# The perceptron's second product made token by token: squares become the stationary operand, weights are streamed

## The chip, the core and the metric

The kernel runs on one core of a Trainium2 chip. The metric is the device time of the whole program in microseconds. Three runs of the kernel before took 3518.9, 3522.17 and 3524.16 us; the median is 3522.17.

The core has five engines that run at the same time, each working off its own list of instructions in order: TensorE (PE in the rows; PEld are its weight loads), VectorE (DVE), ScalarE (ACT), GpSimd (POOL) and SyncE (SP), which issues the transfers. They wait for each other through semaphores.

## What is computed

Input `x` is 16 sequences of 1024 tokens with 256 values each. Two layers follow each other, each a layer norm, an attention `s` and a gate `g`, added as `x + s * silu(g)`. The first layer is a recurrent gated linear attention with a mixture of experts as gate, the second a windowed attention with a perceptron as gate. The change is in that perceptron only:

```python
def _bitlinear(x, w_latent):
    scale = clip(mean(abs(w_latent), axis=1, keepdims=True), 1e-05, None)
    tern = clip(round(w_latent / scale), -1.0, 1.0)
    return x @ (tern * scale).T            # forward value

h = _bitlinear(x, w_fc) + gate * (x @ v.T @ fast_b.T @ u.T)
r = maximum(h, 0.0)
return _bitlinear(r * r, w_proj)           # w_proj: (256, 1024)
```

Its result, 256 values for each token, goes through silu and is multiplied by the attention's output.

## The kernel before

A loop runs over the 16 sequences, eight of them unrolled in its body. The next sequence's first steps (layer norm, turning, low-rank and query products: the `head_...` helpers) are woven into the end of the current one. P is 128, D 256, KD = D/P = 2, MT = 8 (tiles of the hidden 1024), NG = 2 (halves of 512 tokens), NC = 8 (chunks of 128 tokens). Arrays are kept "turned" (features on the partitions, tokens along the row) where TensorE is to sum over features, and by token where values are normalised, gated and stored.

The perceptron is a loop over n = 0 to 15, that is over half g = n // 8 and hidden tile m = n % 8, and each engine has its own copy of it, written out by hand, several steps apart:

- TensorE: `hidden(n)` (L1837) makes hidden tile m for 512 tokens in a bank (4 matmuls of a high and a low part, one of rank 16). Three steps later `project(n - 3)` (L1861) adds this tile's share to the 256 outputs, held turned in banks 5 and 6, one per 128 outputs. Between them stand steps of the next sequence's head. The last three `project` stand behind the loop, among `head_project`, `head_route` and `head_queries`.
- ScalarE: `relus(n)` (L1089) from the bank to SBUF with the first weights' scale, then `squares(n - 1)` (L1068), the rounding of the square to fp32r, `sq_hi`.
- GpSimd: the square itself (L847).
- VectorE: `sq_lo = sq - sq_hi` (L1448), and between these `head_stats`, `head_normalise` (two chunks each at n = 6 to 9), `head_low_split`, and `finish2`.

When half g is summed up, ScalarE's `ffn_scaled(g)` (L1074, at n = 10 for the first half, behind the loop for the second) copies banks 5 and 6 to `ft` with the scale of the second weights, which is one number per output, that is per partition of the turned result. TensorE's `ffn_turn(c)` (L1876) turns `ft` back by token, two transposes for each chunk of 128 tokens, at n = 11 to 14 for the first half and among `head_queries` for the second. ScalarE's `ffn_tanh(c)` (L1082) and VectorE's `finish2(c)` (L1424: `f_gates`, `sf`, `x`) read the turned bank and complete the chunk, and SyncE stores it.

Two guards matter later. `project(8)`, the first of the second half, overwrites banks 5 and 6 and waits for both parts of `ft`. And at the next sequence's start TensorE's turning of `gates` (L1541) overwrites banks 0 and 1 and waits until ScalarE has done `experts_relu(0)` and `(1)` (L887); ScalarE gets to those behind the last `ffn_tanh`, the exponentials and logarithms of L870 and L879, and two copies. GpSimd's first step of a sequence, `parity_queries(0)` (L753), waits for `head_queries_out(1)` on ScalarE (L449). VectorE's end of a sequence runs: `head_gate` 0 to 2 (L457), `head_logits`, `head_gate(3)`, `finish2(4)`, `finish2(5)`, `head_top`, `finish2(6)`, `head_index`, `finish2(7)`.

Of the kernel before, what the change touches and what calls it, by code (L numbers as in the profile page):

```python
# [16 lines left out]
ALU = mybir.AluOpType  # L17
# [26 lines left out]
BIG = -1e30  # L44
DV = 2 * DH
UNROLL = 8


def build_program(nc, a, out, n_seq):
# [115 lines left out]
    scale_pj = sb("scale_pj", [P, KD])  # L165
    thr = sb("thr", [P, 2, MT])
# [33 lines left out]
    ft = kt[:, :, 0:512]  # L200
# [74 lines left out]
    for k in range(KD):  # L275
# [11 lines left out]
             "relu_ok sq_ok sqh_ok sql_ok pj_ok ft_ok ftp_ok tf2_ok f3_ok f4_ok y2_ok gkh_ok gkl_ok nst_ok nve_ok nrs_ok "  # L287
# [14 lines left out]
    for count, signals in (  # L302
# [4 lines left out]
            (4, "gkl_ok ve2 rs2 zexp_ok zln_ok qk2_ok xt_ok ft_ok zabs_ok gk_ok gkh_ok v2_ok z_ok "  # L307
# [7 lines left out]
             "cum_ok vg_ok f_ok ot_ok otok_ok ytp_ok s_ok pv_ok xp_ok o2tp_ok s2p_ok ftp_ok"),  # L315
# [21 lines left out]
    ffn_banks = (4, 7, 4, 7, 2, 3, 2, 3)  # L337

# [73 lines left out]
    def head_project(pe, p, where="body"):  # L412

        pe.wait_ge(s["zlo_ok"], at("zlo_ok", p // 2 + 1))
        if where == "before":
            pe.wait_ge(s["xt_ok"], at("xt_ok", NC // 2))
        elif p == 3:
            pe.wait_ge(s["f3_ok"], at("f3_ok", 4))
        else:
            pe.wait_ge(s["relu_ok"], at("relu_ok", NG * MT - 2 + p))  # L420
# [14 lines left out]
    def head_queries(pe, half, where="body"):  # L435

        if half:
            pe.wait_ge(s["z_ok"], at("z_ok", 3))
        elif where == "body":
            pe.wait_ge(s["f3_ok"], at("f3_ok", 3))  # L440
# [36 lines left out]
    with nc.Block() as block:  # L477
# [61 lines left out]
        def _(dve):  # L539
# [15 lines left out]
            for nat, ter, scale, n, width in ((fc_nat[:], fc_ter, scale_fc, MT, D), (pj_nat, pj_ter, scale_pj, KD, HID)):  # L555
# [5 lines left out]
                for m in range(n):  # L561
                    link(nc.vector.tensor_scalar(ter[:, m, :], nat[:, m, :], thr[:, 1, m:m + 1], None, ALU.is_lt))
                    link(nc.vector.scalar_tensor_tensor(ter[:, m, :], nat[:, m, :], thr[:, 0, m:m + 1],
                                                        ter[:, m, :], ALU.is_gt, ALU.subtract))
            link(nc.vector.reciprocal(rscale[:], scale_fc[:]))
# [54 lines left out]
    with nc.Block() as block:  # L620

        @block.tensor
        def _(pe):
# [17 lines left out]
            for m in range(0, MT, 4):  # L641
                turn([u_st[:, m + j, :] for j in range(4)])

        @block.scalar
        def _(act):
# [3 lines left out]
            for n, target in enumerate(targets):  # L649
                act.wait_ge(tern_pe, n + 1)  # L650
                nc.scalar.copy(target, bank[2 + n % 4][:]).then_inc(tern_act, 1)

# [58 lines left out]
    with nc.Fori(0, n_seq // UNROLL) as turn:  # L711
        with nc.Block() as block:
# [141 lines left out]
            def _(act):  # L854
                for copy in range(UNROLL):
# [218 lines left out]
                    def ffn_scaled(g):  # L1074
                        act.wait_ge(s["pj_ok"], at("pj_ok", (g + 1) * MT))
                        if g:
                            act.wait_ge(s["ftp_ok"], at("ftp_ok", 4 * g))
                        for o in range(KD):
                            nc.scalar.activation(ft[:, o, :], bank[5 + o][:], ACT.Identity, scale=scale_pj[:, o:o + 1])\
                              .then_inc(s["ft_ok"], 1)  # L1080

                    def ffn_tanh(c):  # L1082
                        act.wait_ge(s["ftp_ok"], at("ftp_ok", c + 1))
                        if c:
                            act.wait_ge(s["f3_ok"], at("f3_ok", c))
                        nc.scalar.activation(tanh_f[:], bank[ffn_banks[c]][:, 0:D], ACT.Tanh, scale=0.5)\
                          .then_inc(s["tf2_ok"], 1)
# [16 lines left out]
                    for n in range(3, NG * MT + 2):  # L1104
# [10 lines left out]
                        if n == MT + 2:  # L1115
                            ffn_scaled(0)
                        if MT + 3 <= n < MT + 7:
                            ffn_tanh(n - MT - 3)
                    ffn_scaled(1)
# [13 lines left out]
            def _(dve):  # L1133
                for copy in range(UNROLL):
# [288 lines left out]

                    def finish2(c):  # L1424
# [4 lines left out]
                        nc.vector.scalar_tensor_tensor(f_gate, tanh_f[:], 1.0, bank[ffn_banks[c]][:, 0:D],  # L1429
# [9 lines left out]
                    for n in range(NG * MT + 1):  # L1439
                        if n == MT + 5:  # L1440
# [28 lines left out]
                    head_logits(dve)  # L1469
                    head_gate(dve, 3)  # L1470
# [9 lines left out]
            def _(pe):  # L1480
                for copy in range(UNROLL):
# [29 lines left out]
                    def experts_down(i):  # L1511
# [10 lines left out]
                        elif i == 2:  # L1522
                            pass
                            if copy:
                                pe.wait_ge(s["f3_ok"], at("f3_ok"))
# [335 lines left out]
                    def project(n):  # L1861
# [113 lines left out]
```

## Time and profile before

| | |
|---|---|
| median of three runs | 3522.17 us |
| the profiled execution | 3520.74 us |
| its span, first to last instruction | 3519.0 us |
| TensorE busy, matmuls | 3365.3 us (96%) |
| TensorE busy, weight loads | 2272.8 us (65%) |
| VectorE busy | 2584.2 us (73%) |
| ScalarE busy | 1868.9 us (53%) |
| GpSimd busy | 1286.4 us (37%) |
| TensorE clock granted, mean | 0.996 of full |

A matmul's duration is the time until its last result is written, and the next one begins before that; so what a matmul costs TensorE is read from the distance between two starts, not from its length. In the same way operations on the other engines start a little before the one ahead has ended. A time "in us from the span's start" is where a row lies; one sequence takes about 213.5 us, and the rows below are from the first one's end and the second one's start.

### The profile page before, as it was taken

The page shows a single profiled execution, that of the slowest core. Times are in us where ns is not written, and L with a number is a line of the kernel's source. Part 1 is how long each engine was busy: PE and PEld are TensorE (multiplying, and loading weights), DVE is VectorE, ACT ScalarE, POOL GpSimd, SP SyncE. Part 2 cuts the span into 40 slices and gives each one's busy share as a digit, 9 for nine tenths or more (in the row PEclk, how much of TensorE's full clock was granted, in tenths as well). Part 3 has the DMA queues.
Part 4 walks back from the last instruction along what each step waited for, and adds up shares of the span by engine and source line. Part 5 has one row for each costly group of instructions (what it writes and reads, how often), then busy time and mean ns, then how long its engine had stood idle before and what let it go on. Part 6 is the DMA issues. An engine that isn't in the chain of part 4 may idle for free. (4 is left out here: it accounts for less than half of the span.)

```text
span 3519.0 us, 89054 instructions
## 1 busy us (share of the span) xinstructions
PE 3365.3 (96%) x34556; PEld 2272.8 (65%) x34556; DVE 2584.2 (73%) x6183; ACT 1868.9 (53%) x4135; POOL 1286.4 (37%) x1473
## 2 busy tenths in 40 slices
PE   3999999999999999999989999999999999999998
PEld 2666666666667666666656666666666666766666
DVE  4777877778677776777767777787777867777677
ACT  2365463645636465464654636556364563646546
POOL 3523335242343423425234252333524234342342
PEclk9999999999999999999999999999999999999999
DMA  3101010010100101101010010101001010010100
GB/s 91 26 23 49 11 46 21 20 48 12 48 18 23 45 23 37 23 25 38 23 38 22 26 37 23 49 11 50 18 20 48 13 47 18 23 45 23 37 23 26
DMA packets 98492, 109.71 MB, mean 31 GB/s; under 512 B 21152, under 2 KB 75024, under 8 KB 98064
## 3 DMA queue, kind: packets, MB, share of 16 engines
q1 hardware_dynamic: 98064, 103.94, 11.3%
q8 instruction: 277, 4.54, 0.5%
q14 instruction: 151, 1.24, 0.1%
HBM read 74.01 MB, written 17.30 MB: 26 GB/s over the span
## 5 line engine op out<-in xcount | busy, mean ns | idle before, releaser
L847 POOL TENSOR_TENSOR qx<-qx 128x512 f32<-128x512 f32 x256 | 278.2, 1091 | 685.0 <-ACT qx L1093 684.1
L1223 DVE TENSOR_TENSOR am<-bank,causal 128x512 f32<-128x512 f32 x512 | 328.2, 683 | 42.2 <-PE bank L1597 42.2
L1448 DVE TENSOR_TENSOR sq_lo<-qx,sq_hi 128x512 fp32r<-128x512 f32 x256 | 207.8, 812 | 193.3 <-ACT sq_hi L1072 192.8
L1356 DVE TENSOR_REDUCE row_max<-bank 128x4 f32<-128x384 f32 x512 | 271.9, 549 | 91.9 <-PE bank L1755 91.9
L968 ACT ACTIVATE tanh_g<-bank 128x256 f32<-128x256 f32 x128 | 49.2, 384 | 405.7 <-PE bank L1486 405.7
L1486 PE MATMUL bank<-w_vg,xt 128*128 128x512 f32 x512 | 252.3, 615 | 0.0
L1527 PE MATMUL bank<-xt,w_down 128*128 128x512 f32 x512 | 237.2, 596 | 0.0
L1871 PE MATMUL bank<-sq_hi,pj_t 128*128 128x512 f32 x512 | 214.4, 419 | 16.4 <-DVE sq_lo L1448 9.8
L1365 DVE TENSOR_TENSOR am<-bank,row_max 128x384 f32<-128x384 f32 x384 | 212.8, 554 | 9.8
L1093 ACT ACTIVATE qx<-bank,scale_fc 128x512 f32<-128x512 f32 x256 | 177.7, 694 | 56.2 <-PE bank L1858 56.2
L1012 ACT ACTIVATE am<-am 128x384 f32<-128x384 f32 x384 | 200.2, 526 | 9.8 <-DVE am L1365 3.3
L1871 PE MATMUL bank<-sq_lo,pj_t 128*128 128x512 f32 x512 | 202.5, 396 | 0.0
L753 POOL TENSOR_TENSOR qx<-qt,par_mask 128x512 f32<-128x512 f32 x128 | 136.1, 1063 | 178.5 <-ACT qt L449 138.4
L1072 ACT CAST sq_hi<-qx 128x512 fp32r<-128x512 f32 x256 | 158.9, 621 | 67.1 <-PE bank L1871 36.7
L1282 DVE TENSOR_TENSOR state_sum<-bank,state_mid 128x256 f32<-128x256 f32 x112 | 47.4, 423 | 179.9 <-PE bank L1711 179.9
L1772 PE MATMUL bank<-ident,am 64*96 64x64 f32 x4096 | 166.9, 221 | 9.7 <-ACT qx L1028 9.2
L1772 PEld LDWEIGHTS bank<-ident,am 64*96 64x96 f32 x4096 | 131.1, 123 | 69.4 <-issue 50.0
L762 POOL TENSOR_SCALAR o_veps<-o_mom 128x1 f32<-128x1 f32 x128 | 37.4, 292 | 372.9 <-DVE o_mom L1303 372.9
L1853 PE MATMUL bank<-xh,fc_t 128*128 128x512 f32 x512 | 171.9, 417 | 0.0
L1755 PE MATMUL bank<-k,qt 32*32 32x192 f32 x8192 | 164.0, 332 | 4.6 <-ACT qt L946 4.6
L1853 PE MATMUL bank<-xl,fc_t 128*128 128x512 f32 x512 | 159.9, 393 | 0.0
L1486 PEld LDWEIGHTS bank<-w_vg,xt 128*128 128x128 f32 x512 | 86.8, 189 | 98.4 <-issue 98.4
(261 smaller groups left out, 8740.0 us busy)
## 6 DMA issues: line engine op xcount, KB each, us to landing
g_wide<-gate_rows SPq DMA_DIRECT2D x64, 512.0 KB, 6.4
qt<-in_L_attn_x SPq DMA_DIRECT2D x136, 128.0 KB, 2.2
x<-in_L_attn_x SPq DMA_DIRECT2D x128, 128.0 KB, 2.2
out<-x SPq DMA_DIRECT2D x128, 128.0 KB, 1.7
k<-k SPq DMA_DIRECT2D x96, 128.0 KB, 2.4
x<-in_L_ffn_w_fc SPq DMA_DIRECT2D x1, 1024.0 KB, 5.8
attn<-in_L_ffn_w_proj SPq DMA_DIRECT2D x1, 1024.0 KB, 8.2
w_up<-in_L_ffn_Wu SPq DMA_DIRECT2D x1, 512.0 KB, 6.0
```

The source lines that it names most:

```text
L847: nc.gpsimd.tensor_tensor(sq[:, n % 3, :], relu[:, n % 3, :], relu[:, n % 3, :], ALU.mult)\
L1012: nc.scalar.activation(pr[:, j], pr[:, j], ACT.Exp).then_inc(s["pr_ok"], 1)
L1093: nc.scalar.activation(relu[:, n % 3, :], bank[1 + n % 3][:], ACT.Relu, scale=scale_fc[:, n % MT:n % MT + 1]).then_inc(s["relu_ok"], 1)
L1223: nc.vector.tensor_tensor(am_tiles[:, :, j], bank[3 + j][:].rearrange("p (f e t) -> p f e t", f=2, e=2), causal[:].unsqueeze(1).unsqueeze( ...
L1356: nc.vector.tensor_reduce(row_max[:, j, :], bank[1 + j][:, 0:4 * KW].rearrange("p (h k) -> p h k", k=KW), AX.X, ALU.max, negate=(j == 0)). ...
L1365: nc.vector.tensor_tensor(pr[:, j], bank[1 + j][:, 0:4 * KW].rearrange("p (h k) -> p h k", k=KW), row_max[:, j, :].unsqueeze(2).broadcast_ ...
L1448: nc.vector.tensor_tensor(sq_lo[:, n % 3, :], sq[:, n % 3, :], sq_hi[:, n % 3, :].bitcast(F32), ALU.subtract)\
L1486: mm = nc.tensor.matmul(dst, xt[:, k, c * P:(c + 1) * P], w[:, k, :], start=(k == 0), stop=(k == KD - 1))
L1527: mm = nc.tensor.matmul(bank[5 if g else j][:], w_down[:, k, j * P:(j + 1) * P], xt[:, k, g * 512:(g + 1) * 512], start=(k == 0), stop=(k ...
L1772: mm = nc.tensor.transpose(bank[5 + r][0:KW, h * QB:(h + 1) * QB], pr[rows, 2 * p + h // 4, h % 4, :], ident[rows, rows])
L1853: nc.tensor.matmul(h_bank, fc_t[:, k, m * P:(m + 1) * P], t[:, g, k, :], start=(t is xh and k == 0), stop=False)
L1871: mm = nc.tensor.matmul(bank[5 + o][:], pj_t[:, m, o * P:(o + 1) * P], part[:, n % 3, :], start=(m == 0 and part is sq_hi), stop=(m == MT ...
```

## The change

The second product is made by token. In `project`, the 128x128 pieces of `sq_hi` and `sq_lo` are the stationary operand and the 256 columns of `pj_t` are streamed, so that banks 5 and 6 hold, by token, two chunks of 256 outputs each. The scale now differs along the row, so it is spread over all partitions once in the set-up (`bc_pj`), and VectorE multiplies (two instructions for each half) in the place of ScalarE's four copies a sequence. `ffn_turn` and its banks go; tanh and `finish2` read `ft` in SBUF. `ft` lies in the other half of `kt`. Some waits of TensorE on `f3_ok` go with the banks.

```diff
-    ft = kt[:, :, 0:512]
+    ft = kt[:, :, 512:S]
+    spread = sf[:].rearrange("p (o t) -> p o t", o=KD)
...
+    def ffn_part(c):
+        return ft[:, c % 4 // 2, c % 2 * D:(c % 2 + 1) * D]
...
# head_project
         if where == "before":
             pe.wait_ge(s["xt_ok"], at("xt_ok", NC // 2))
-        elif p == 3:
-            pe.wait_ge(s["f3_ok"], at("f3_ok", 4))
-        else:
+        elif p < 3:
             pe.wait_ge(s["relu_ok"], at("relu_ok", NG * MT - 2 + p))
...
# head_queries
-        elif where == "body":
-            pe.wait_ge(s["f3_ok"], at("f3_ok", 3))
...
# set-up: VectorE, TensorE, ScalarE
+            for o in range(KD):
+                link(nc.vector.tensor_copy(spread[:, o, :], scale_pj[:, o:o + 1].broadcast_to([P, P])))
...
+            turn([spread[:, o, :] for o in range(KD)])
...
+            act.wait_ge(tern_pe, len(targets) + 1)
+            nc.scalar.copy(bc_pj[:], bank[2 + len(targets) % 4][:, 0:D]).then_inc(tern_act, 1)
...
# ScalarE
-                    def ffn_scaled(g):
-                        act.wait_ge(s["pj_ok"], at("pj_ok", (g + 1) * MT))
-                        if g:
-                            act.wait_ge(s["ftp_ok"], at("ftp_ok", 4 * g))
-                        for o in range(KD):
-                            nc.scalar.activation(ft[:, o, :], bank[5 + o][:], ACT.Identity, scale=scale_pj[:, o:o + 1])\
-                              .then_inc(s["ft_ok"], 1)
-
                     def ffn_tanh(c):
-                        act.wait_ge(s["ftp_ok"], at("ftp_ok", c + 1))
+                        act.wait_ge(s["ft_ok"], at("ft_ok", c // 2 + 1))
                         if c:
                             act.wait_ge(s["f3_ok"], at("f3_ok", c))
-                        nc.scalar.activation(tanh_f[:], bank[ffn_banks[c]][:, 0:D], ACT.Tanh, scale=0.5)\
-                          .then_inc(s["tf2_ok"], 1)
+                        nc.scalar.activation(tanh_f[:], ffn_part(c), ACT.Tanh, scale=0.5).then_inc(s["tf2_ok"], 1)
...
-                        if n == MT + 2:
-                            ffn_scaled(0)
                         if MT + 3 <= n < MT + 7:
                             ffn_tanh(n - MT - 3)
-                    ffn_scaled(1)
...
# VectorE
+                    def ffn_scaled(g):
+                        dve.wait_ge(s["pj_ok"], at("pj_ok", (g + 1) * MT))
+                        if g:
+                            dve.wait_ge(s["f3_ok"], at("f3_ok", 4))
+                        for half in range(2):
+                            nc.vector.tensor_tensor(ft[:, half, :].rearrange("p (a d) -> p a d", d=D),
+                                                    bank[5 + half][:].rearrange("p (a d) -> p a d", d=D),
+                                                    bc_pj[:].unsqueeze(1).broadcast_to([P, 2, D]), ALU.mult)\
+                              .then_inc(s["ft_ok"], 1)
...
-                        nc.vector.scalar_tensor_tensor(f_gate, tanh_f[:], 1.0, bank[ffn_banks[c]][:, 0:D],
+                        nc.vector.scalar_tensor_tensor(f_gate, tanh_f[:], 1.0, ffn_part(c),
...
                     for n in range(NG * MT + 1):
+                        if n == MT + 2:
+                            ffn_scaled(0)
                         if n == MT + 5:
                             head_low_split(dve, 0)
...
                     head_logits(dve)
+                    ffn_scaled(1)
                     head_gate(dve, 3)
                     finish2(4)
...
# TensorE
-                        elif i == 2:
-                            pass
-                            if copy:
-                                pe.wait_ge(s["f3_ok"], at("f3_ok"))
...
-                        for o in range(KD):
+                        for a in range(4):
+                            out = bank[5 + a // 2][:, a % 2 * D:(a % 2 + 1) * D]
                             for part in (sq_hi, sq_lo):
-                                mm = nc.tensor.matmul(bank[5 + o][:], pj_t[:, m, o * P:(o + 1) * P], part[:, n % 3, :],
-                                                      start=(m == 0 and part is sq_hi),
+                                mm = nc.tensor.matmul(out, part[:, n % 3, a * P:(a + 1) * P], pj_t[:, m, :],
+                                                      start=(m == 0 and a % 2 == 0 and part is sq_hi),
                                                       stop=(m == MT - 1 and part is sq_lo), skip_group_check=True)
                         mm.then_inc(s["pj_ok"], 1)
-
-                    def ffn_turn(c):
...
-                        if MT + 3 <= n < MT + 7:
-                            ffn_turn(n - MT - 3)
...
                     head_queries(pe, 0)
-                    ffn_turn(4)
-                    ffn_turn(5)
                     head_queries(pe, 1)
-                    ffn_turn(6)
-                    ffn_turn(7)
```

## Rows read from the trace of the kernel before

**Rows 1.** Two whole sequences: stretch, length, busy us (instructions) of each engine, clock, DMA

```profile
290.60:504.20 213.60, 208.69 (x2156) 140.94 (x2155) 159.25 (x380) 115.92 (x257) 78.57 (x87) 1.00 0.11 30
504.20:717.70 213.50, 208.63 (x2156) 140.89 (x2155) 159.19 (x380) 115.92 (x257) 78.57 (x87) 1.00 0.12 30
```

**Rows 2.** Sums of waits: engine and line, released by: us in total, times, longest

```profile
PEld bank L1871 <- DVE sq_lo L1448: 37.2, 81, 0.7
```

**Rows 3.** Timeline of TensorE (start us, length us): one whole project, to the next one's start

```profile
285.42 0.39 PE L1871 MATMUL bank<-sq_hi,pj_t 128*128 128x512 f32 x1
...
286.35 0.63 PE L423 MATMUL bank<-gk_st,z_st 128*128 128x256 f32 x4
```

**Rows 4.** Timeline: matmuls of 256 columns, and eight weight loads behind each other

```profile
288.42 0.97 PEld L431 LDWEIGHTS bank<-gk_st,z_st 128*128 128x128 f32 x8 [0.30 <-DVE z_st L409]
...
311.23 0.28 PE L1555 MATMUL bank<-xl,cumulator 128*128 128x256 f32 x1
...
311.71 0.28 PE L1555 MATMUL bank<-xl,cumulator 128*128 128x256 f32 x1
```

**Rows 5.** Timeline of TensorE around the first pair of turns

```profile
271.61 0.39 PE L1871 MATMUL bank<-sq_lo,pj_t 128*128 128x512 f32 x1
271.85 0.38 PE L1885 MATMUL bank<-ident,k 128*128 128x128 f32 x2
...
272.53 0.62 PE L1853 MATMUL bank<-xl,fc_t 128*128 128x512 f32 x2
```

**Rows 6.** Timeline where the first half of the tokens is scaled

```profile
268.57 0.40 PE L1871 MATMUL bank<-sq_lo,pj_t 128*128 128x512 f32 x1
...
268.87 1.45 DVE L368 TENSOR_SCALAR xn<-qt,moments,rstd 128x256 f32<-128x256 f32 x2
...
269.42 1.28 ACT L1079 ACTIVATE k<-bank,scale_pj 128x512 f32<-128x512 f32 x2
...
270.24 0.68 DVE L1448 TENSOR_TENSOR sq_lo<-qx,sq_hi 128x512 fp32r<-128x512 f32 x1
...
270.81 0.19 PEld L1871 LDWEIGHTS bank<-sq_hi,pj_t 128*128 128x128 f32 x1 [0.55 <-issue]
...
270.84 0.73 DVE L368 TENSOR_SCALAR xn<-qt,moments,rstd 128x256 f32<-128x256 f32 x2
```

**Rows 7.** Bank times tile on VectorE: count, ns least/median/most

```profile
L457 DVE TENSOR_TENSOR am<-bank,bc_gk x68: 680/683/693, 69.1 to 3508.4; 128x512 f32<-128x512 f32 x68
...
L1223 DVE TENSOR_TENSOR am<-bank,causal x512: 678/683/692, 103.1 to 3394.0; 128x512 f32<-128x512 f32 x171
```

**Rows 8.** Timeline of a sequence's end

```profile
292.18 0.68 DVE L457 TENSOR_TENSOR am<-bank,bc_gk 128x512 f32<-128x512 f32 x1
...
293.39 0.42 DVE L1429 SCALAR_TENSOR_TENSOR f_gates<-tanh_f,bank 128x256 f32<-128x256 f32 x1 [0.52 <-ACT tanh_f L1086]
...
294.69 0.87 PE L1885 MATMUL bank<-ident,k 128*128 128x128 f32 x4
...
295.39 3.60 PE L1507 MATMUL bank<-xt,w_k 128*128 128x512 f32 x8
...
295.97 0.60 ACT L449 COPY qt<-bank 128x512 f32<-128x512 f32 x1
...
296.64 1.04 POOL L753 TENSOR_TENSOR qx<-qt,par_mask 128x512 f32<-128x512 f32 x1 [9.89 <-ACT qt L449]
296.66 0.41 DVE L1429 SCALAR_TENSOR_TENSOR f_gates<-tanh_f,bank 128x256 f32<-128x256 f32 x1
...
297.10 0.86 DVE L1434 SCALAR_TENSOR_TENSOR sf<-f_gates,attn 128x256 f32<-128x256 f32 x1
297.16 0.38 ACT L1086 ACTIVATE tanh_f<-bank 128x256 f32<-128x256 f32 x1 [0.60 <-DVE f_gates L1429]
```

**Rows 9.** Timeline of the next sequence's start, where TensorE turns the gates

```profile
304.09 1.25 ACT L887 ACTIVATE qx<-bank,b_down 128x512 f32<-128x512 f32 x2
...
305.44 1.05 PEld L1541 LDWEIGHTS bank<-ident,gates 128*128 128x128 f32 x8 [0.42 <-issue]
305.69 1.04 PE L1541 MATMUL bank<-ident,gates 128*128 128x128 f32 x8
```

More of the change, by code:

```diff
@@ L44 @@
 BIG = -1e30
+UNROLL = 8
 DV = 2 * DH
-UNROLL = 8
 def build_program(nc, a, out, n_seq):
@@ L165, in build_program @@
     scale_pj = sb("scale_pj", [P, KD])
+    bc_pj = sb("bc_pj", [P, D])
     thr = sb("thr", [P, 2, MT])
@@ L286, in build_program @@
              "pr_ok ptp_ok pt_ok ptd_ok pv_ok oc_ok xp_ok rden_ok o2_ok o2tp_ok o2t_ok s2p_ok s2_ok xh_ok xl_ok tp_ok thi_ok tst_ok h2p_ok "
-             "relu_ok sq_ok sqh_ok sql_ok pj_ok ft_ok ftp_ok tf2_ok f3_ok f4_ok y2_ok gkh_ok gkl_ok nst_ok nve_ok nrs_ok "
+             "relu_ok sq_ok sqh_ok sql_ok pj_ok ft_ok tf2_ok f3_ok f4_ok y2_ok gkh_ok gkl_ok nst_ok nve_ok nrs_ok "
              "nxn_ok hqp_ok hqk_ok").split()
@@ L306, in build_program @@
             (3, "kh_ok"),
-            (4, "gkl_ok ve2 rs2 zexp_ok zln_ok qk2_ok xt_ok ft_ok zabs_ok gk_ok gkh_ok v2_ok z_ok "
+            (4, "gkl_ok ve2 rs2 zexp_ok zln_ok qk2_ok xt_ok zabs_ok gk_ok gkh_ok v2_ok ft_ok z_ok "
              "qk2p_ok v2p_ok xtp_ok zp_ok"),
@@ L314, in build_program @@
              "y_ok f2_ok x_ok xn2_ok ptd_ok rden_ok o2_ok s2_ok nxn_ok f3_ok f4_ok y2_ok hp_ok "
-             "cum_ok vg_ok f_ok ot_ok otok_ok ytp_ok s_ok pv_ok xp_ok o2tp_ok s2p_ok ftp_ok"),
+             "cum_ok vg_ok f_ok ot_ok otok_ok ytp_ok s_ok pv_ok xp_ok o2tp_ok s2p_ok"),
             (16, "sq_ok relu_ok sqh_ok ost_ok st2 sql_ok nst_ok h2p_ok pj_ok x_in"),
@@ L336, in build_program @@
     head_query_banks = (4, 1)
-    ffn_banks = (4, 7, 4, 7, 2, 3, 2, 3)
+    def ffn_part(c):
+        return ft[:, c % 4 // 2, c % 2 * D:(c % 2 + 1) * D]
     def head_load(sp, index):
@@ L1868, in project @@
                             pe.wait_ge(s["ft_ok"], at("ft_ok", KD))
-                        for o in range(KD):
+                        for a in range(4):
+                            out = bank[5 + a // 2][:, a % 2 * D:(a % 2 + 1) * D]
                             for part in (sq_hi, sq_lo):
-                                mm = nc.tensor.matmul(bank[5 + o][:], pj_t[:, m, o * P:(o + 1) * P], part[:, n % 3, :],
-                                                      start=(m == 0 and part is sq_hi),
+                                mm = nc.tensor.matmul(out, part[:, n % 3, a * P:(a + 1) * P], pj_t[:, m, :],
+                                                      start=(m == 0 and a % 2 == 0 and part is sq_hi),
                                                       stop=(m == MT - 1 and part is sq_lo), skip_group_check=True)
                         mm.then_inc(s["pj_ok"], 1)
-                    def ffn_turn(c):
-                        if c % 4 == 0:
-                            pe.wait_ge(s["ft_ok"], at("ft_ok", KD * (c // 4 + 1)))
-                        if c in (4, 5):
-                            pe.wait_ge(s["z_ok"], at("z_ok", c - 3))
-                        elif c >= 2:
-                            pe.wait_ge(s["f3_ok"], at("f3_ok", c - 1))
-                        j = c % 4
-                        for k in range(KD):
-                            mm = nc.tensor.transpose(bank[ffn_banks[c]][:, k * P:(k + 1) * P],
-                                                     ft[:, k, j * P:(j + 1) * P], ident[:])
-                        mm.then_inc(s["ftp_ok"], 1)
                     pe.wait_ge(s["qk2_ok"], at("qk2_ok", 3))
```

## The prediction

> **What bounds the kernel now.** First the busy time of the engines in two whole sequences [rows 1]: of 213.6 us TensorE is busy 208.7, VectorE 159.3, ScalarE 115.9. The two stretches are alike to 0.1 us, so one sequence can be read and multiplied by 16. TensorE's clock is granted in full (1.00, the 2.4 GHz level). Then the sums of the waits [rows 2]: TensorE's weight loads for the second product waited for `sq_lo` 81 times, 37.2 us in all, 2.3 us a sequence. Elsewhere little is lost, so TensorE's own order of work bounds the kernel, and a microsecond on it counts in full, unless the edit lets another engine arrive last. So I read three timelines: the product itself, the change from the first to the second half of 512 tokens, and the end of a sequence with the start of the next.
>
> **The products.** Before, a `project` is 4 matmuls of 512 columns; a whole one goes from 285.42 to 286.35, 0.93 us, 0.233 each [rows 3]. After, it is 8 matmuls of 256 columns, each with a fresh 128x128 weight load. The trace has this shape at L1554/1555 (the same hi/lo pair, both operands of the same kind): five starts span 311.23 to 311.71, 0.12 us each [rows 4]. Eight make 0.96. Difference +0.03 us for each of 16 projects, +0.48 a sequence. The waits for `sq_lo` [rows 2], where nothing is gained by arriving early, swallow part of it: I take **+0.3**, between 0 and +0.48.
>
> The Trainium skill, "TensorE: Matmul & The Clock Gate", section "Part 3: Packing small matmuls — row/col tiling", says a weight load overlaps matmuls in flight only when the row groups differ; here all use all 128 rows, so it speaks against doubling the loads. The trace does not agree: full 128-row pairs follow each other at 0.12 us [rows 4].
>
> **Turns removed inside the loop.** `ffn_turn(0)` to `(3)` stand on TensorE's path. The last 512-column matmul ahead of one starts at 271.61 and ends its turn of 0.233 at 271.85; the third matmul of `hidden(12)` starts at 272.53, so its first started at 272.53 - 2 x 0.233 = 272.07 [rows 5]. One pair of transposes is 0.22 us; four are **-0.88**.
>
> **The scaling of the first half moves from ScalarE to VectorE, with a queue ahead of it.** This is the largest term. `project(8)` waits for both parts of `ft`, as it overwrites banks 5 and 6. Before, ScalarE starts scaling at 269.42, soon after the last matmul of `project(7)` (start 268.57, 0.40 long), and ends at 270.70; TensorE loads the weights of `project(8)` at 270.81, after 0.55 us without a load, so a small stall is there already [rows 6]. After, `ffn_scaled(0)` is written on VectorE at n = 10, that is behind `sq_lo(9)` and behind the normalising of chunks 6 and 7. VectorE gets there late: 1.45 us for chunks 4 and 5 from 268.87, `sq_lo(9)` at 270.24, chunks 6 and 7 at 270.84 for 0.73 us [rows 6]. The starts of back-to-back operations lie 0.07 us before the end of the one ahead, so scaling starts at 271.50. One product of a bank with a broadcast row of 128x512 has its twin in `head_gate`, L457: 683 ns, 680 to 693 in 68 cases [rows 7]; starts are 0.60 to 0.61 apart [rows 6]. Two parts end at 271.50 + 0.61 + 0.68 = 272.79, and with the 0.11 us from release to load [rows 6] TensorE goes on at 272.90 instead of 270.81: **+2.1**. The relief of ScalarE by 1.28 us buys nothing here, because TensorE stands at `project(8)` and gives it no work. GpSimd squares beside it, but L1223, also bank times tile, never took over 692 ns in 512 cases [rows 7]. Bounds: +1.3 if VectorE reached it at 270.7, by chunks 6 and 7 going faster and less contention before them; +2.6 if a product were held up by GpSimd for half a microsecond. `sq_lo(10)` is put back to 272.7, but is wanted only at `project(10)`, 277.7 in the timeline, and TensorE will be later itself; nothing.
>
> **The end of a sequence.** Turns 4 to 7 go: two of them, between `head_queries` 0 and 1, cost TensorE 2 x 0.22 = 0.44 [rows 5], and two, with a wait, 295.39 - 294.69 = 0.70 ahead of the next sequence [rows 8]. That would be -1.14, but the chain that ends last becomes another one. TensorE next needs at L1541 that ScalarE has done two `experts_relu` (banks 0 and 1 free). They end at 304.09 + 1.25 = 305.34, and L1541's load starts at 305.44, its matmul at 305.69 [rows 9]: only 0.1 us of slack today. Ahead of them ScalarE works without a break from `ffn_tanh(7)` at 297.16 [rows 8], and that waits for `f_gates` of chunk 6 on VectorE, 296.66. VectorE's tail is a queue. Before: `head_gate(3)` at 292.18, idle 0.52, chunk 4 at 293.39, chunk 6 at 296.66. After: the two products take 292.18 and 292.79, `head_gate(3)` 293.40, chunk 4 at 294.01, its tanh ready, so the idle time is gone, and chunk 6 at 294.01 + 3.27 = 297.28: +0.62. ScalarE, L1541's release and so TensorE come 0.62 later, less the 0.1 of slack: **+0.5**, and TensorE, though 1.14 earlier in its own queue, idles about 1.5 us there.
>
> A second cost is near a tie. `f_gates` now reads `tanh_f` and `ft`, both in SBUF, where before one operand was a bank. GpSimd's `parity_queries(0)`, 1.04 us, starts 0.07 after `head_queries_out(1)` [rows 8]. The VectorE operation with two SBUF operands that met it, L1434 at 297.10, took 0.86 instead of 0.42. That copy starts 2.58 after chunk 4's first operation (295.97 against 293.39), and ScalarE's steps between keep their lengths: after, 294.01 + 2.58 + 0.60 + 0.07 = 297.26 for GpSimd, against 297.28 for `f_gates` of chunk 6. If GpSimd is first, `f_gates` waits till 298.3 and the whole chain is 0.9 later. Too close to call; I take half, **+0.4**, and keep 0 and +0.9.
>
> The Trainium skill, "SBUF — State Buffer", section "SBUF: two separate sides", calls the pair of ports that VectorE and GpSimd share an exclusive lock, also for a VectorE operation with two SBUF inputs. L1434 agrees (0.86 against 0.42 us) [rows 8]; by that rule bank-reading products stay free.
>
> **At no cost.** The set-up adds two small copies, two transposes and one copy, once, while the engines wait for loads; uncovered under 1 us once. `head_project(3)`, `head_queries(0)` and `experts_down(2)` lose waits that had long been met. `ft` in the other half of `kt` is free until well into the next sequence.
>
> **Sum** a sequence: +0.3 - 0.88 + 2.1 + 0.5 + 0.4 = +2.4 us; by 16, +39 us. The profiled execution took 3520.74 (span 3519.0 and 1.7 around it); its sum is 3560, and the median of the runs, 3522.17, is 1.4 above it. Predicted: **3560 us**. With each term at its bounds: low 0 - 0.88 + 1.3 + 0.5 + 0 = +0.9, 3535; high 0.48 - 0.88 + 2.6 + 0.5 + 0.9 = +3.6, 3578.
>
> **Rivals.**
> 1. *VectorE keeps up, and the turns are won (faster).* If VectorE reached `ffn_scaled(0)` before about 269.4, the scaling would be ready by 270.7 and `project(8)` no later than now; and if the tail of VectorE were no longer, all of the turns would come off: 0.3 - 0.88 - 1.14 = -1.7, 3493 us. Its point of decision is VectorE's arrival at 269.4 and at 292.2; for it speaks that VectorE is idle a quarter of the sequence, against it that its queue in these two places is full [rows 6, 8]. Chance 7%.
> 2. *Only one of the two places bites (about the same).* Stall without tail: 0.3 - 0.88 + 2.1 - 1.14 = +0.4, 3527; tail without stall: 0.3 - 0.88 + 0.5 = -0.1, 3520. Chance 9%.
> 3. *Weight loads are not hidden (much slower).* A bare load follows the next at (0.97 - 0.19) / 7 = 0.111 us [rows 4]; four more in the open in each of 256 projects are +114 us on the sum, 3674. Against it the 0.12 us spacing. By the page named above this is what would come. Chance 3%.
>
> The forecast has 81%.
>
> **Range.** 3532 to 3578 holds nearly all of the forecast; the rivals are left out. Within 0.2% (about what a measurement can tell, 7 us) means 3515 to 3529. Faster 0.07, same 0.10, slower 0.83.
>
> **What would show it.** Right: eight matmuls of `project` 0.12 us apart; `project(8)` released by VectorE's `ft`, with a gap of some 2.4 us ahead of it in every sequence; a wait of about 1.5 us at L1541's successor on ScalarE's `experts_relu`; no transposes of `ft`; the period from 213.5 to about 216 us. Wrong: if the gap ahead of `project(8)` is below 1 us, VectorE arrived sooner than its queue here says; if the matmuls stand 0.2 us apart, the loads are exposed; if L1541's successor doesn't wait, the tail was not VectorE's.

## The result, and the profile of the kernel after

The changed kernel takes **3555.62 us** (median of 4 runs, 3552.77 to 3556.42); the kernel before, on the same chip, 3521.89. The ratio is 1.0096, with a 95% interval of 1.0081 to 1.0111. The forecast was 3560, range 3532 to 3578. The profiled execution took 3552.77 us (before 3520.74).

A regular sequence of the kernel after: the stretch, its length, then busy us (instructions) of PE, PEld, DVE, ACT, POOL, then the granted clock, the DMA share and the rate. It answers to [rows 1]. The length of a regular sequence, from one landmark to the same one in the next sequence, is called the period below.

```profile
286.10:501.20 215.10, 206.67 (x2204) 142.36 (x2202) 161.34 (x383) 114.09 (x253) 78.73 (x87) 1.00 0.11 30
```

TensorE is busy 2 us less (the turns are gone) in a sequence that is 1.6 us longer: what it won it stands idle, and more. The sums of the waits say where (engine, operation and line, released by; us in all, times, longest):

```profile
PE bank L1874 <- DVE k L1422: 37.3, 16, 2.4
PEld bank L1874 <- DVE sq_lo L1453: 32.6, 69, 0.7
PE bank L1543 <- ACT qx L892: 19.3, 14, 1.4
```

The first is the second product waiting for VectorE's scaling (L1422; the rows call `ft` `k`), once a sequence and 2.33 us each; in the kernel before, the same place waited 0.27 us for ScalarE's. The third is the turning of the gates waiting for ScalarE's `experts_relu`; in the kernel before, that wait stood in two sequences only, 0.6 us each (VectorE's `gdiff`, ahead of `f_gates`, took 1.04 us there in place of 0.17, beside GpSimd's `parity_queries(0)`). The wait for `sq_lo` [rows 2] has shrunk from 37.2 to 32.6 us.

The first place on the timeline (start, length, engine, line, operation; in brackets the idle time before it and what ended it). It answers to [rows 6]:

```profile
269.44 1.46 DVE L372 TENSOR_SCALAR xn<-qt,moments,rstd 128x256 f32<-128x256 f32 x2
270.81 0.68 DVE L1453 TENSOR_TENSOR sq_lo<-qx,sq_hi 128x512 fp32r<-128x512 f32 x1
271.41 0.72 DVE L372 TENSOR_SCALAR xn<-qt,moments,rstd 128x256 f32<-128x256 f32 x2
272.06 1.28 DVE L1422 TENSOR_TENSOR k<-bank,bc_pj 128x512 f32<-128x512 f32 x2
...
270.67 0.48 PE L1860 MATMUL bank<-t_st,u_t 128*128 128x512 f32 x1
273.48 0.36 PE L1874 MATMUL bank<-pj_t,sq_hi 128*128 128x256 f32 x1 [2.34 <-DVE k L1422]
273.68 0.28 PE L1874 MATMUL bank<-pj_t,sq_lo 128*128 128x256 f32 x1
```

VectorE comes to the two products only at 272.06, behind two pairs of normalisings and `sq_lo(9)`, and TensorE starts `project(8)` 0.11 us after it could. The second place answers to [rows 9]:

```profile
302.90 3.60 PE L1513 MATMUL bank<-xt,w_q 128*128 128x512 f32 x8
307.87 1.07 PE L1543 MATMUL bank<-ident,gates 128*128 128x128 f32 x8 [1.37 <-ACT qx L892]
```

The same landmarks in one regular sequence of each timeline, by the starts of TensorE's matmuls there (differences by subtraction):

| from | to | before | after | difference | forecast |
|---|---|---|---|---|---|
| `head_queries(0)`, 504.42 / 508.07 | first attention step, 528.96 / 533.03 | 24.54 | 24.96 | +0.42 | +0.5, +0.4 for the tie |
| there | `project(5)`, 689.71 / 693.74 | 160.75 | 160.71 | -0.04 | some of the products |
| there | `project(8)`, 697.94 / 704.04 | 8.23 | 10.30 | +2.07 | +2.1, some of the products |
| there | next `head_queries(0)`, 717.92 / 723.19 | 19.98 | 19.15 | -0.83 | -0.88, some of the products |
| sum | | 213.50 | 215.12 | +1.62 | +2.4 |

Fourteen regular sequences at +1.6 are 22 us. The rest of the 32 between the two profiled executions lies in three places: the first sequence (some +2), the one in which the program's loop goes round (225.8 before, 229.0 after, +3.2), and two stretches in which TensorE's clock fell to 0.50 for 3.4 us (about +1.7 each). What is left, about 1 us, is in periods that are 0.1 to 0.3 longer than 215.1 and in the end. A sequence in which the loop goes round has a long stretch at half clock in both kernels, 10.2 us before and 13.7 after; the 3.4 us more are about what makes its +3.2 out of a regular +1.6. The first sequence holds 10.2 us at half clock before and 17.1 after, while e7 below, nearly the same program, has 10.2 and ends it 2.0 us sooner (290.56 against 292.61); so its +2 need not come from the change either.

### The profile page after: what moved, and what is told of

The parts are those of the page before. It is cut to its first block and busy times, and to the rows that moved or that the text cites. A ratio compares the mean times of both kernels' runs of the same rounds, so it can differ in the third digit from the quotient of the medians.

```text
span 3551.1 us, 90549 instructions
## 1 busy us (share of the span) xinstructions
PE 3343.2 (94%) x35326; PEld 2299.1 (65%) x35326; DVE 2622.9 (74%) x6249; ACT 1838.2 (52%) x4072; POOL 1293.4 (36%) x1473
## 5 line engine op out<-in xcount | busy, mean ns | idle before, releaser
L1874 PE MATMUL bank<-pj_t,sq_hi 128*128 128x256 f32 x1024 | 263.9, 291 | 48.0 <-DVE k L1422 37.3
L1874 PE MATMUL bank<-pj_t,sq_lo 128*128 128x256 f32 x1024 | 251.2, 279 | 0.0
L1874 PEld LDWEIGHTS bank<-pj_t,sq_hi 128*128 128x128 f32 x1024 | 192.3, 188 | 86.8 <-issue 49.5
L1358 DVE TENSOR_TENSOR am<-bank,row_max 128x384 f32<-128x384 f32 x384 | 212.8, 554 | 9.8
L1874 PEld LDWEIGHTS bank<-pj_t,sq_lo 128*128 128x128 f32 x1024 | 192.3, 188 | 3.8
```

The lines of the kernel that those rows point to most:

```text
L1358: nc.vector.tensor_tensor(pr[:, j], bank[1 + j][:, 0:4 * KW].rearrange("p (h k) -> p h k", k=KW), row_max[:, j, :].unsqueeze(2).broadcast_ ...
L1874: mm = nc.tensor.matmul(out, part[:, n % 3, a * P:(a + 1) * P], pj_t[:, m, :], start=(m == 0 and a % 2 == 0 and part is sq_hi), stop=(m == ...
```

## The experiments

Two theories stand against each other wherever the price may come from: that TensorE waits for VectorE in the two places, and that the new form of the product itself costs time (weight loads) or VectorE meets GpSimd.

### The form of the product alone: e1_split_columns

The kernel before, with each 512-column matmul of `project` as two of 256 columns, so that there are as many fresh weight loads as in the change (8 a `project`), and nothing else.

```diff
-    for o in range(KD):
+    for o, h in ((0, 0), (0, 1), (1, 0), (1, 1)):
+        cols = slice(h * D, (h + 1) * D)
         for part in (sq_hi, sq_lo):
-            mm = nc.tensor.matmul(bank[5 + o][:], pj_t[:, m, o * P:(o + 1) * P], part[:, n % 3, :],
+            mm = nc.tensor.matmul(bank[5 + o][:, cols], pj_t[:, m, o * P:(o + 1) * P], part[:, n % 3, cols],
...
```

> The kernel before, with each matmul of 512 columns in project cut into two of 256 (the weights stay pj_t, the result stays turned): the shape of the change's product alone, eight loads and eight matmuls of 256 columns in place of four of 512. Theory (loads hidden): starts 0.117 to 0.120 us apart, so a project takes 0.94 to 0.96 us instead of 0.93, and the time is 0 to 5 us above the kernel before, ratio 1.000 to 1.0015. Rival (each further load stands in the open for 0.11 us): 0.44 us more in each of 256 projects, +110 us, ratio 1.03.

Measured: 3520.13, ratio 0.9998 (0.9989 to 1.0007). The added loads cost nothing that can be measured, and rival 3 (+114 us) falls. The matmuls stand as in the kernel after (here from e1):

```profile
282.96 0.28 PE L1872 MATMUL bank<-sq_hi,pj_t 128*128 128x256 f32 x1
283.07 0.28 PE L1872 MATMUL bank<-sq_lo,pj_t 128*128 128x256 f32 x1
...
284.66 0.28 PE L1872 MATMUL bank<-sq_lo,pj_t 128*128 128x256 f32 x1
```

Sixteen starts span 1.70 us, 0.113 each: half of the 0.233 of a 512-column one [rows 3], or a little less. What e1 doesn't have of the change is the swap of the operands, squares loaded and weights streamed; that is read from the trace of the kernel after. From the first matmul of a `project` to what follows it, the median at full clock is 0.944 us before, 0.946 in e1 and 0.945 after. So the product's form costs nothing, against the +0.3 of the sum. The Trainium skill, "TensorE: Matmul & The Clock Gate", section "Part 3: Packing small matmuls — row/col tiling", has one line by which a load overlaps matmuls in flight only where the row groups differ (further up, the same section also lets a load into the background weight buffer go ahead); the experiment decides against that line for this shape, where every load uses all 128 rows.

### Only the scaling moved: e2_scale_on_vector

The kernel before with its turns and its form of the product, but `ffn_scaled` written on VectorE at the change's two places (scale by partition, so with `tensor_scalar`).

```diff
 # VectorE
+    nc.vector.tensor_scalar(ft[:, o, :], bank[5 + o][:], scale_pj[:, o:o + 1], None, ALU.mult)
...
+        if n == MT + 2:
+            ffn_scaled(0)
...
     head_logits(dve)
+    ffn_scaled(1)
     head_gate(dve, 3)
```

> The kernel before, with nothing changed but who scales: VectorE multiplies the turned banks by the scale of each partition, at the places in its order where the change puts it; product and turns stay. Theory (VectorE's order is what costs): project(8) goes on 2.1 us later than before, and at the end of a sequence the turns wait for VectorE, about 1.0 us more; 3.1 us a sequence, +50 us, ratio 1.014. Rival (the product by token costs, not the place of the scaling): no difference beyond 5 us.

Measured: 3593.74, ratio 1.0207 (1.0191 to 1.0223), more than expected. The mechanism is the expected one:

```profile
270.02 1.40 DVE L1418 TENSOR_SCALAR k<-bank,scale_pj 128x512 f32<-128x512 f32 x2
271.57 0.47 PE L1871 MATMUL bank<-sq_hi,pj_t 128*128 128x512 f32 x1 [2.47 <-DVE k L1418]
...
294.34 0.66 PE L1885 MATMUL bank<-ident,k 128*128 128x128 f32 x4 [0.95 <-DVE k L1418]
```

A gap of 2.47 us ahead of `project(8)` and one of 0.95 at the turns of the second half. But the period is 218.4, 4.9 above 213.5, where the two waits explain about 3.2. The rest is the clock. Windows of e2 from just ahead of a later `project(8)`, which starts at 488.34 after a gap of 2.47 (after the window its length, then as above; the clock is the third number from the end):

```profile
486.00:488.00 2.00, 0.00 (x0) 0.00 (x0) 2.00 (x5) 1.35 (x3) 1.04 (x1) 1.00 0.00 0
488.00:490.00 2.00, 1.66 (x7) 1.42 (x8) 0.79 (x2) 0.00 (x0) 0.00 (x0) 0.82 0.00 0
490.00:492.00 2.00, 2.00 (x6) 1.49 (x5) 1.27 (x3) 0.39 (x1) 0.00 (x0) 0.50 0.00 0
492.00:494.00 2.00, 2.00 (x5) 0.89 (x4) 0.00 (x0) 0.00 (x0) 0.00 (x0) 0.83 0.19 66
```

The granted clock falls from 1.00 to 0.50 (2.4 to 1.2 GHz) soon after the gap and stays there for 3.4 us, in which work of 1.7 us is done: another +1.7, in 14 of the 16 sequences. Such a stretch is called a half-clock stretch below. The gap of the kernel after is nearly as long (2.34), yet one followed it only twice.

### VectorE's queue ahead of the first half: e3_scale_early

The kernel after, with `ffn_scaled(0)` written at n = 8, behind `sq_lo(8)` and ahead of the normalising of that iteration.

```diff
-        if n == MT + 2:
-            ffn_scaled(0)
...
+        if n == MT:
+            ffn_scaled(0)
```

> The changed kernel with ffn_scaled(0) moved in VectorE's order from n = 10 to n = 8, behind sq_lo(8) and ahead of the normalising of chunks 4 to 7. Theory (TensorE's gap of 2.6 us ahead of project(8) is VectorE's queue, not its work): the gap shrinks to about 0.2, 2.4 us a sequence come off, -39 us: 3516, ratio to the kernel before 0.9985. Rival (the added work on VectorE is what costs, wherever it stands): the time stays at 3555, ratio 1.0096.

Measured: 3509.42, ratio 0.9966 (0.9952 to 0.9979): 46 us less than the kernel after, by moving two instructions.

```profile
269.49 1.29 DVE L1422 TENSOR_TENSOR k<-bank,bc_pj 128x512 f32<-128x512 f32 x2
270.70 0.73 DVE L372 TENSOR_SCALAR xn<-qt,moments,rstd 128x256 f32<-128x256 f32 x2
...
270.90 0.19 PEld L1874 LDWEIGHTS bank<-pj_t,sq_hi 128*128 128x128 f32 x1 [0.15 <-issue]
```

The gap of 2.62 us between the loads has become 0.15, even less than the 0.55 before [rows 6]. The period is 212.8, 2.3 below that of the kernel after. Sixteen times 2.3 is 37 us, and the two half-clock stretches, which are gone, give 3; the rest of the 42 us between the two profiled executions (3552.77 and 3510.86) is in periods of the kernel after that are a little longer than 215.1. That the stall comes from VectorE's order of work, not from its load, is shown here. It is also rival 2's second case, tail without stall, forecast at 3520: it came out 11 lower, as the products cost nothing and the small stall of before went too.

### The same products twice: e5_first_half_twice, e6_second_half_twice

The kernel after, each product of one half done once more ahead of the real one, into a buffer that nobody reads: VectorE is 1.2 to 1.3 us later in that one place. Nothing of the output's work is left out.

```diff
         for half in range(2):
+            if g == 0:          # e6: g == 1
+                nc.vector.tensor_tensor(kt[:, half, 0:512]..., bank[5 + half]..., bc_pj..., ALU.mult)
             nc.vector.tensor_tensor(ft[:, half, :]..., bank[5 + half]..., bc_pj..., ALU.mult)
```

> The changed kernel, with both products of ffn_scaled(0) done twice (first into a part of kt that is not in use), the cost of the first half's scaling on VectorE doubled and nothing else. Theory (project(8) is released by the end of VectorE's queue): the gap ahead of project(8) grows by the two products' 1.2 us, 16 times: +19 us, 3575, ratio to the kernel before 1.015. Rival 1 (cover is left there): under 3 us more. Rival 2 (a longer gap also brings a stretch of TensorE's clock at half in every sequence, as where VectorE scaled the turned banks, 1.7 us each): 3602, ratio 1.023.

Measured for e5: 3588.25, ratio 1.0192 (1.0175 to 1.0209), between the theory and its second rival.

```profile
709.99 0.55 PE L1878 MATMUL bank<-pj_t,sq_hi 128*128 128x256 f32 x1 [3.53 <-DVE k L1426]
...
708.00:710.00 2.00, 0.01 (x1) 0.04 (x1) 2.00 (x5) 0.42 (x1) 0.56 (x1) 0.64 0.00 0
710.00:712.00 2.00, 2.00 (x9) 2.00 (x10) 1.63 (x4) 0.00 (x0) 0.00 (x0) 0.50 0.04 8
```

The gap grew from 2.34 to 3.53, by 1.19, and so did the period (216.3) in the sequences whose clock stayed at 1.00. At 12 of the 16 gaps the clock fell to 0.50, for 3.4 us and once, at the gap shown, for 6.8; here it fell before the gap had ended. With 3.4 us the period is 218.0. Both effects are there: the wait counts one for one, and on top of it comes 1.7 us where the clock falls.

> The changed kernel, with both products of ffn_scaled(1) done twice in the same way, at the end of a sequence. Theory (the chain of VectorE's queue, the last tanh and ScalarE's queue releases the turning of the gates, though TensorE is long ready): the wait there grows by 1.2 us: +19 us, 3575, ratio 1.015. Rival (the idle 1.4 us of TensorE there are slack that the chain can use): no change, 3555, ratio 1.0096.

Measured for e6: 3590.71, ratio 1.0194 (1.0177 to 1.0211).

```profile
520.28 3.60 PE L1517 MATMUL bank<-xt,w_q 128*128 128x512 f32 x8
525.89 1.06 PE L1547 MATMUL bank<-ident,gates 128*128 128x128 f32 x8 [2.01 <-ACT qx L892]
...
528.00:530.00 2.00, 2.00 (x4) 0.88 (x3) 1.97 (x3) 0.00 (x0) 1.64 (x2) 0.50 0.13 43
```

The wait at the turning of the gates grew from 1.37 to 2.01, and 12.6 us ahead of it, at the next sequence's first matmuls, TensorE now waits 0.29 us for VectorE's products (at 513.31). From `head_queries(0)` to the turning of the gates it is 16.46 us, against 15.26 in the kernel after: the whole 1.2. The clock fell behind the wait in each of the 14 sequences that have it, and four times at the gap ahead of `project(8)` as well. Periods are 218.0 with one such stretch, 219.5 with two. So VectorE's tail has no slack in the kernel after: what it is late there, TensorE waits. Without its half-clock stretch a period of 218.0 would be 216.3, which is the +1.2 of the added work.

### The tie of VectorE and GpSimd: e7_vector_later, e10_vector_later_2

The prediction put a price of 0.9 us on `f_gates` of chunk 6 coming just after GpSimd's `parity_queries(0)`. In the kernel after it came just before, in all fourteen sequences:

```profile
299.02 0.42 DVE L1432 SCALAR_TENSOR_TENSOR f_gates<-tanh_f,k 128x256 f32<-128x256 f32 x1
299.06 1.27 POOL L758 TENSOR_TENSOR qx<-qt,par_mask 128x512 f32<-128x512 f32 x1 [10.53 <-ACT qt L449]
299.48 1.14 DVE L1437 SCALAR_TENSOR_TENSOR sf<-f_gates,attn 128x256 f32<-128x256 f32 x1
```

Both experiments add a write to a buffer that nobody reads, so that VectorE is the later one:

```diff
     head_top(dve)
+    nc.vector.memset(tie[:], 0.0)               # e7: 64 columns
+    nc.vector.memset(kt[:, 0, 0:384], 0.0)      # e10: 384 columns
     finish2(6)
```

> The changed kernel with a small write of 128x64 zeros on VectorE, 0.1 to 0.2 us, ahead of f_gates of chunk 6, so that GpSimd's parity_queries(0), which now starts 0.04 us behind f_gates, starts ahead of it. Theory (an operation of VectorE with two SBUF operands waits until GpSimd's is done; the +0.4 of my sum was half of this): f_gates ends some 1.0 us later, and so does the next turning of the gates: +12 to 16 us, 3570, ratio 1.0137. Rival (f_gates isn't held up): +0.1 to 0.2 us a sequence, 3558, ratio 1.0103.

Measured for e7: 3555.69, ratio 1.0096 (1.0079 to 1.0113). The write was swallowed by the pause ahead of `f_gates` (297.06 against 297.02 for GpSimd): VectorE was 0.04 us later than GpSimd and no more. `f_gates` took 0.36 us and wasn't held, here and in twelve of the fourteen sequences. Whether 0.04 was enough is left open by these, so the write was made longer.

> The changed kernel with a write of 128x384 zeros on VectorE (in e7_vector_later the write of 128x64 was swallowed by the operation ahead, and f_gates came no later) ahead of f_gates of chunk 6, so that GpSimd's parity_queries(0) is well under way when f_gates comes up, some 0.3 to 0.4 us later than now. Theory (an operation of VectorE with two SBUF operands waits for GpSimd's): f_gates ends with GpSimd's operation, 0.9 to 1.0 us later than now, and the next turning of the gates too; +14 us or more, 3570, ratio 1.0136. Rival (no hold): only the write's own 0.3 to 0.4 us: +5 to 6 us, 3561, ratio 1.011.

Measured for e10: 3564.31, ratio 1.0124 (1.0109 to 1.014), between the two again.

```profile
513.10 1.62 POOL L758 TENSOR_TENSOR qx<-qt,par_mask 128x512 f32<-128x512 f32 x1 [10.53 <-ACT qt L449]
513.18 0.38 DVE L1480 MEMSET k<- 128x384 f32 x1
513.47 0.36 DVE L1432 SCALAR_TENSOR_TENSOR f_gates<-tanh_f,k 128x256 f32<-128x256 f32 x1
513.87 1.14 DVE L1437 SCALAR_TENSOR_TENSOR sf<-f_gates,attn 128x256 f32<-128x256 f32 x1
```

`f_gates` starts 0.37 us after GpSimd's operation and still takes 0.36; instead GpSimd's record grew from 1.27 to 1.62, and the next operation, `sf`, was held, as without the write. So it is in twelve of the fourteen sequences; their period is 215.5, +0.4, which is the write itself. In the other two it went as the theory says, with the same starts:

```profile
1594.28 1.04 POOL L758 TENSOR_TENSOR qx<-qt,par_mask 128x512 f32<-128x512 f32 x1 [10.53 <-ACT qt L449]
1594.35 0.38 DVE L1480 MEMSET k<- 128x384 f32 x1
1594.65 0.95 DVE L1432 SCALAR_TENSOR_TENSOR f_gates<-tanh_f,k 128x256 f32<-128x256 f32 x1
...
1604.04 1.06 PE L1544 MATMUL bank<-ident,gates 128*128 128x128 f32 x8 [2.32 <-ACT qx L892]
```

GpSimd's operation takes 1.04, `f_gates` is held (0.95), and TensorE's wait at the turning of the gates is 2.32 us in place of 1.72. The same two sequences of e7, the seventh of each eight, have `f_gates` 0.3 us behind GpSimd, at 1.01 and 1.00 us long, and the wait at 2.31 in place of 1.39: the 0.9 us of the prediction. What sets these two apart wasn't tried. Seven half-clock stretches in place of two are most of the rest of e10's time. So the price of the tie is real, but coming second by the records' starts doesn't decide who pays it. The added write is itself an operation of VectorE, 0.07 us behind GpSimd's start, and may be what kept GpSimd waiting in the twelve; no run here separates the two. Another `f_gates` of the kernel after was held, for 1.15 us at 283.95, where TensorE doesn't wait for it.

The Trainium skill, "SBUF — State Buffer", section "🔬 SBUF: two separate sides", says that whichever of the two starts first holds the shared ports for its whole instruction. By the starts in the records the two sequences of e10 agree with that and the twelve do not, with GpSimd 0.07 us ahead of the write and 0.37 us ahead of an unhindered `f_gates`; whether GpSimd's access begins as early as its record, no run here can show.

### What limits the tail: e4, e8, e11

Three orders on top of e3. e4 moves VectorE's `head_top` behind `finish2(6)`:

```diff
-    head_top(dve)
     finish2(6)
+    head_top(dve)
```

> As e3_scale_early, and at the end of a sequence head_top (0.76 us of VectorE) is moved behind finish2(6), out of the way of f_gates of chunk 6, for which the last tanh waits. Theory (the end of a sequence is bound by VectorE's queue, then ScalarE's, with TensorE idle some 1.4 us at the turning of the gates): another 0.76 us a sequence come off, -12 us: 3504, ratio 0.995. Rival (the wait of TensorE there is covered, or another chain is as late): the same time as e3_scale_early.

Measured: 3510.65, ratio 0.9971 (0.996 to 0.9982), no better than e3. The wait at L1543 shrank to 0.90 us, but another came later, at the first `experts_up`:

```profile
530.54 1.99 PE L1627 MATMUL bank<-w_up,qx 128*128 128x256 f32 x8 [0.36 <-POOL qx L804]
```

e8 leaves `head_top` and changes ScalarE's order: `first_queries_keys(2)` and `(3)` behind the first two `experts_relu`, the copies of the gates' rows ahead of `(4)` and `(5)`.

```diff
-    first_queries_keys(2)
-    first_queries_keys(3)
...
     experts_relu(0)
     experts_relu(1)
-    first_queries_keys(4)
-    first_queries_keys(5)
+    first_queries_keys(2)
+    first_queries_keys(3)
     for b in range(NG):
...
+    first_queries_keys(4)
+    first_queries_keys(5)
```

> As e3_scale_early, and on ScalarE the copies first_queries_keys(2) and (3), 1.05 us, are moved behind experts_relu(0) and (1), and (4) and (5) behind the copies of the gates' rows. Theory (what is left at the start of a sequence is ScalarE's queue: both the turning of the gates and, behind it, GpSimd's first gating, which waits for the transfer of those rows, come out of it): both come 1.05 us earlier, TensorE's idle 1.38 us shrink to 0.3, -16 us against e3_scale_early: 3494, ratio 0.992. Rival (as where head_top was moved: another chain, from VectorE over GpSimd, ends as late): the time stays at that of e3_scale_early, 0.9966.

Measured: **3502.59**, ratio 0.9947 (0.993 to 0.9963), the fastest of all, 53 us below the kernel after and 19 below the kernel before, but not the 3494 expected. Its rows:

```profile
515.12 1.06 PE L1543 MATMUL bank<-ident,gates 128*128 128x128 f32 x8 [0.42 <-ACT qx L890]
...
527.01 1.27 POOL L804 TENSOR_TENSOR qx<-qx,g_wide 128x512 f32<-128x512 f32 x1 [4.49 <-DMA g_wide<-gate_rows]
528.33 1.99 PE L1627 MATMUL bank<-w_up,qx 128*128 128x256 f32 x8 [0.26 <-POOL qx L804]
```

The wait at L1543 gave 0.96 us (1.38 in e3, 0.42 here), the mean period only 0.4 (212.8 to 212.4). The wait at L1627, 0.26 us in the sequence shown, goes from nothing to 1.5 us and is 0.41 in the mean of the fourteen. Behind it stands the way of the gates' rows out to memory and back as `g_wide`: GpSimd's product waits 4.5 us for it and `experts_up` for that. This is a chain of transfers that TensorE's haste doesn't shorten.

e11 is e8 with `head_top` late as in e4 and the copies of the gates' rows between `first_queries_keys(2)` and `(3)` (the diff is against e8).

```diff
     experts_relu(0)
     experts_relu(1)
     first_queries_keys(2)
-    first_queries_keys(3)
     for b in range(NG):
...
+    first_queries_keys(3)
     first_queries_keys(4)
```

> e8_early_and_copies_late with head_top behind finish2(6) (as in e4_early_and_top_late) and the copies of the gates' rows ahead of first_queries_keys(3). Theory (two waits were left there: TensorE's 0.42 us for ScalarE at the turning of the gates, and 0.26 us at experts_up(0) for GpSimd, which waits for the transfer of those rows; head_top alone only moved the wait from the one to the other, so both have to go): 0.4 to 0.6 us a sequence below e8_early_and_copies_late, 3493 to 3496, ratio 0.992. Rival (what head_top yields is given back at experts_up(0) again): the time stays at 3502, 0.9947.

Measured: 3509.9, ratio 0.9971 (0.9959 to 0.9983). There is no wait of the matmuls at L1543 any more, and one at L1627 in every sequence, 1.2 us in the mean; the shortest but one:

```profile
529.46 1.99 PE L1627 MATMUL bank<-w_up,qx 128*128 128x256 f32 x8 [0.47 <-POOL qx L804]
```

The new limit is the same as in e8, but e11 is 7 us slower, with a mean period of 212.8. Both theories missed that. One sequence misleads here, because the way of the gates' rows varies by up to 2 us between the sequences of one run; so the fourteen regular ones are averaged. From GpSimd's `parity_queries(0)` to its first product with `g_wide` it is 19.85 us in e3 and 19.87 in e8, but 20.25 in e4 and 20.24 in e11. The order of ScalarE doesn't move it; `head_top` behind `finish2(6)`, which e4 and e11 share, makes it 0.4 longer both times. That is also where e11 loses against e8: counted from `head_queries(0)`, its `experts_up(0)` (L1627) starts at 28.02 in place of 27.65, and from there to the end of the sequence the two run alike. `head_top` yields time to the last tanh and takes it from the gates' rows. Which step between `head_top` and the transfers makes the 0.4 wasn't traced.

## Why the prediction was right, point by point

- **What bounds the kernel.** That TensorE's own order does, so that an operation taken off counts only where no other engine arrives last: the turns in the loop are gone in full (-0.83), and yet the kernel is slower.
- **The stall ahead of `project(8)`** (+2.1): measured +2.07, gap 2.34 where some 2.4 was forecast. Adding up VectorE's queue by the starts of back-to-back operations was enough (the 0.60 between the starts of two products is not in [rows 6], but holds: two of them take 1.28 here, 0.60 and 0.68): forecast 2.93 us behind the last matmul of `project(7)`, measured 272.06 - 269.28 = 2.78. e3 shows that it is this queue.
- **The tail** (+0.5): measured +0.42; the wait at the turning of the gates is 1.37, forecast about 1.5. Chunk 6's `f_gates` came 299.02 - 295.76 = 3.26 after chunk 4's, as in [rows 8] (3.27). e6 shows that this tail has no slack; e8, that ScalarE's part of it could be ordered otherwise, which the prediction didn't look at.
- **The turns in the loop** (-0.88): -0.83 between `project(8)` and the next `head_queries(0)`, with the products of that stretch in it.
- **The products** (+0.3) were mis-sized: 0. The 0.12 us read from five starts was rounded up; over sixteen matmuls the difference to half of 0.233 nearly vanishes (286.27 to 288.15 is 1.88 for sixteen, 0.94 a `project` against 0.93), over all of them it is gone, and e1 times the doubled loads at nothing.
- **The tie** (+0.4, half of 0.9) came out at 0, as it fell to the free side: `f_gates` was 0.04 us ahead in all fourteen sequences, where the prediction had it 0.02 behind. The order was called rightly as too close. What stood behind the price, the reading of L1434 in [rows 8] as "the later one waits", holds only in part: of the sequences of e7 and e10 in which `f_gates` is the later one, two of fourteen in each pay (0.9 and 0.6 us), and twelve don't.
- **Left out of the sum**: the one half-clock stretch more where the loop goes round (+1.6 beyond a regular sequence), two half-clock stretches elsewhere (+3.4), and 1 to 2 us in the first sequence, the end and a few longer periods. Together some 6 us. The sum of +39 had sixteen sequences at +2.4; two terms of it were too high (0.7 a sequence, 11 us), the others by 0.1 together (1.6 us), and the 6 us left out bring what remains, +26, to the +32 measured. That 3560 lies so near 3555.6 is thus in part luck: the two errors have opposite signs.
- **The rivals**: 3 fell by e1. The second case of 2, tail without stall, is what e3 makes of the change: with VectorE's arrival at the scaling at 269.49 the stall is gone, and the kernel is on the other side of the one before. Its first case (stall without tail) and rival 1 (neither) were not built.

## What to carry to other kernels

When work moves to an engine that is idle a quarter of the time, what counts is where in its queue it stands: here the same two instructions cost 2.3 us a sequence behind five short ones and nothing ahead of them, and the sign of the whole change hung on it. Add up the receiving engine's queue at the place where the result is wanted, put the moved work ahead of anything that is wanted later, and look for what is next in line at each wait that goes (here the transfer of the gates' rows). Average over the sequences before a small difference is put down to a place: one sequence of e11 looked better than it was. Waits of 2.0 to 3.5 us on TensorE could cost more than their length here, as the clock often fell with them.

## What the runs showed of the hardware

The clock. A stretch of 3.4 us at the 1.2 GHz level stood at the TensorE gap in 14 of 16 sequences of e2 (gap 2.47), in 12 of 16 of e5 (3.53, once 6.8 us long), and in all 14 of e6 that wait at the turning of the gates (2.01, in a place with other work behind it), but only twice in the kernel after, whose gap is 2.34. One of the two:

```profile
1565.10 0.36 PE L1874 MATMUL bank<-pj_t,sq_hi 128*128 128x256 f32 x1 [2.34 <-DVE k L1422]
...
1564.00:1566.00 2.00, 0.90 (x7) 0.93 (x8) 1.97 (x5) 0.67 (x2) 0.86 (x1) 1.00 0.00 0
1566.00:1568.00 2.00, 2.00 (x8) 1.61 (x7) 0.78 (x2) 0.00 (x0) 0.00 (x0) 0.56 0.14 49
```

Each costs 1.7 us. In the kernels without a gap of 2 us (before, e3, e8) the regular sequences have none. Where the loop goes round every kernel has one longer stretch, here before and after (clock 0.74 and 0.66 over 20 us; by the clock's own records 10.2 and 13.7 us at half); TensorE's share of the work was low there:

```profile
1790.00:1810.00 20.00, 9.49 (x22) 4.20 (x21) 8.58 (x51) 8.44 (x16) 1.04 (x1) 0.74 0.28 84
1805.00:1825.00 20.00, 7.52 (x12) 3.33 (x13) 8.98 (x51) 7.09 (x15) 1.04 (x1) 0.66 0.28 84
```

The length of the gap alone doesn't say when the clock falls: 2.01 us did it in e6, 2.34 mostly didn't in the kernel after. What else decides it wasn't tried.
